# Two stage borders of a four-layer graph kernel are overlapped: load with the first similarity, the mix's last step with the last similarity

## The reference, cut to what matters

```python
# layers 0 and 3: xn is x transposed to (512, 64, 128)
x_norm = xn / jnp.maximum(jnp.linalg.norm(xn, axis=-1, keepdims=True), 1e-12)
mean_sim = jnp.einsum('nbl,mbl->nm', x_norm, x_norm) / B      # 512 x 512, summed over 64 batches
_, idx = jax.lax.top_k(mean_sim, k + 1)                       # k = 153 neighbours of each row are kept
A = jnp.where(mask, mean_sim, 0); An = dinv[:, None] * A * dinv[None, :]
out = jnp.einsum('sd,sbl->dbl', An, jnp.einsum('nbl,lo->nbo', xn, weight)) + bias
...
# layer 1: tokens are mixed by adj * adj; layer 2, for each batch of 128 tokens:
A_l = relu(zn @ zn.T) * not_eye;  A_g = exp(-d2 / (2 sigma^2)) * not_eye     # both times adj, rows normed
out = (w_l * K_l + (1 - w_l) * K_g) @ v @ W_O.T
```

## Time and profile before

| what | us |
|---|---|
| device time, median of 3 runs (1420.53 to 1422.23) | 1421.34 |
| the profiled execution, device time | 1420.99 |
| its span on the core | 1419.3 |
| busy PE, of the span | 1313.2 |
| busy DVE | 1081.6 |
| busy ACT | 818.8 |
| busy POOL | 566.3 |

### The profile page before, as it was taken

How to read it: one execution, slowest core, us unless ns; L and a number is a source line. 1 busy time by engine, 2 the same in 40 slices (tenths; PEclk the granted TensorE clock), 3 DMA queues, 4 the chain that set the end, 5 groups by cost and what they waited for, 6 DMA issues and landing times. The chain is left out here.

```text
span 1419.3 us, 29584 instructions
## 1 busy us (share of the span) xinstructions
PE 1313.2 (93%) x8776; PEld 726.5 (51%) x8806; DVE 1081.6 (76%) x2169; ACT 818.8 (58%) x1366; POOL 566.3 (40%) x866
## 2 busy tenths in 40 slices
PE   6689988999999889999999999999947997999997
PEld 2156555555555345555555555555514567455553
DVE  0498777888888847888888888888788988356664
ACT  5634345787777633555555555555445446477776
POOL 2100114787787711222222222222222001688887
PEclk9999987999999889999999999999988998999999
DMA  8756200000000022112211111222205440122222
GB/s 325 266 189 210 89 0 1 1 0 0 0 0 0 12 49 38 38 38 38 38 37 37 37 37 37 43 39 39 36 13 177 161 136 1 45 90 81 81 81 97
DMA packets 122971, 93.62 MB, mean 66 GB/s; under 512 B 87712, under 2 KB 87840, under 8 KB 122912
## 3 DMA queue, kind: packets, MB, share of 16 engines
q1 hardware_dynamic: 122720, 92.81, 22.7%
q0 software_dynamic: 192, 0.08, 0.0%
HBM read 54.86 MB, written 17.04 MB: 51 GB/s over the span
## 5 line engine op out<-in xcount | busy, mean ns | idle before, releaser
L546 PE MATMUL pair<-unit_lo,unit_hi 128*128 128x512 f16 x512 | 178.8, 386 | 29.5 <-ACT unit_hi L617 24.7
L2030 POOL TENSOR_TENSOR sq_lo<-sq,sq_hi 128x512 f16<-128x512 f32 x60 | 69.6, 1160 | 139.2 <-ACT sq_hi L1803 139.2
L550 PE MATMUL diag<-unit_hi 128*128 128x128 f16 x512 | 113.4, 221 | 0.0
L548 PE MATMUL pair<-unit_hi 128*128 128x384 f16 (+2 forms) x384 | 106.4, 277 | 0.0
L1150 PE MATMUL po<-an_h,xwh 128*128 128x512 f16 x256 | 98.0, 383 | 0.0
L1151 PE MATMUL po<-an_l,xwh 128*128 128x512 f16 x256 | 97.9, 382 | 0.0
L1152 PE MATMUL po<-an_h,xwl 128*128 128x512 f16 x256 | 97.8, 382 | 0.0
L1785 PE MATMUL work<-m_h,xT 128*128 128x512 f16 x256 | 97.0, 379 | 0.0
L1786 PE MATMUL work<-m_l,xT 128*128 128x512 f16 x256 | 97.0, 379 | 0.0
L1787 PE MATMUL work<-m_h,xT 128*128 128x512 f16 x256 | 97.0, 379 | 0.0
L1089 POOL TENSOR_TENSOR x_all<-x_all,t 128x512 f32 (+1 forms) x64 | 81.2, 1269 | 16.8 <-ACT t L983 12.1
(11 more groups left out here) (438 smaller groups left out, 4237.7 us busy)
## 6 DMA issues: line engine op xcount, KB each, us to landing
x_all<-in_x_dram SPq DMA_DIRECT2D x16, 1024.0 KB, 14.5
tl<-rn_rows SPq DMA_DIRECT2D x64, 256.0 KB, 3.7
sim<-rn_rows SPq DMA_DIRECT2D x64, 256.0 KB, 3.7
out_dram<-x_all SPq DMA_DIRECT2D x64, 256.0 KB, 2.0
weights_a<-in_L_gnn_W_lang_dram SPq DMA_DIRECT2D x1, 1024.0 KB, 11.4
weights_b<-in_L_gnn_W_grav_dram SPq DMA_DIRECT2D x1, 1024.0 KB, 8.3
weights_a<-in_L_gnn_W_O_dram SPq DMA_DIRECT2D x1, 1024.0 KB, 10.6
an_h<-in_L_gnn_W_V_dram SPq DMA_DIRECT2D x1, 512.0 KB, 5.6
```

What stands on the lines that cost most here:

```text
L546: nc.tensor.matmul(pair[i][:], stat, lo[:, r, :], start=first, stop=False, skip_group_check=True)
L548: nc.tensor.matmul(pair[i][:, (i + 1) * P:], stat, hi[:, r, (i + 1) * P:], start=False, stop=final, skip_group_check=True)
L550: last = nc.tensor.matmul(diag[:, i * P:(i + 1) * P], stat, stat, start=(first and i == 0), stop=final, skip_group_check=True)
```

## The change

- **Load and the first similarity are one block** (`load_and_compare`), with no meeting between them. Of each of the parts 6 to 15, POOL squares one batch of four (as a product of x with itself). The root of the early scales is taken one part earlier. The rows of scales, wo, wv and wg are loaded in another order.
- **In both similarities (class `Similarity`) half of the lo parts, the odd batches of a round, go from DVE to POOL** (`lo_on_pool`).
- **The greatest sum (`greatest`) is found by POOL after its last lo part**; before it stood ahead of the middle of the similarity.
- **Step 16 of the mix becomes `closing`**: the 64 grams of layer 3 with the rest of the mix between them. The first four units and hi parts stand inside step 15, and so do the early scales (LATE = 3: groups 13 to 15 are late). The norm statistics of group 14 move from step 15 into closing, and its norm and squares stand behind the grams' rounds 4 and 5; group 15's outputs are PE's work ahead of round 5, its statistics stand around round 6, its norm and squares around round 7. Late scales are stored by SP instead of POOL.
- Buffers and banks are shared accordingly. The meeting with `release_semaphores` that stood between load and similarity and the one between mix and similarity go; one stands between layer 3's similarity and its neighbours, where before there was only the end of a block.

In the diff the last piece is DVE's order in the new step 16; where a line repeats what the list says it is left out.

```diff
-LATE = 2
+LATE = 3
...
+    def units(self, dve, base, start=False):
+        for r in range(self.R):
+            self.take_unit(dve, base, r, start)
+        for r in range(0, self.R, 2 if self.shared else 1):
+            self.lo_on_vector(dve, base, r, start)
...
+    def lo_on_pool(self, pool, base, start=False):
+        for r in range(1, self.R, 2):
...
+    def greatest(self, pool):
+        pool.wait_ge(self.late.top, 1)
+        pool.partition_all_reduce(self.k.s(NSQ_MAX), self.k.s(NSQ_MAX), P, RMAX).then_inc(self.gmax_all, 1)
...
+                early.store(sp)
+                early.all_stored(sp)
+                for base in range(0, B // 2, R):
+                    sim.load(sp, base)
...
+                def closing():
+                    ks = Kernels(NG - 1)
+                    for r in range(0, R, 2):
+                        sim.lo_on_vector(dve, 0, r, True)
+                    ks.add_turned()
+                    sim.units(dve, R)
+                    ks.mask_gravity()
+                    ks.sums()
+                    sim.units(dve, 2 * R)
+                    ks.factors()
+                    ks.mix()
+                    sim.units(dve, 3 * R)
+                    kernels_lo(NG - 1)
+                    moments(NG - 2, range(0, 2))
+                    sim.units(dve, 4 * R)
+                    moments(NG - 2, range(2, G))
+                    sim.units(dve, 5 * R)
+                    add_outputs(NG - 1, (pgg, pbc, pgg, pbc), range(G))
+                    dve.wait_ge(o_u, NG * G)
+                    last.moments(dve, range(0, 2))
+                    sim.units(dve, 6 * R)
+                    last.moments(dve, range(2, G))
+                    sim.units(dve, 7 * R)
...
+                    sim.units(dve, 9 * R)
+                    dve.wait_ge(last.sums, 1)
+                    sim.late.clamp(dve)
+                    sim.units(dve, 10 * R)
+                    sim.late.invert(dve)
+                    sim.units(dve, 11 * R)
+                    sim.late.refine(dve)
```

More of the change, by code:

```diff
@@ L467, in _ @@
                         mix.lang.sum_squares(pe)
+                pe.wait_ge(mix.lang.tmp_r, C)
+                pe.wait_ge(mix.lang.q_in, 1)
+                for r in range(R):
+                    sim.gram(pe, 0, r, r == 0, False)
+                with strided(pe, R, B - R, R) as base:
+                    sim.grams(pe, base)
+                sim.grams(pe, B - R, True)
             @block.vector
@@ L1615, in scratch_tiles, with kernel_mix @@
     return h[:, 0:N], h[:, N:2 * N], l[:, 0:N]
-def select_neighbours(k, rows_bank, scale, layer, mix, ops, ahead=None, last=None):
-    with ExitStack() as banks:
-        pair, diag = similarity(k, banks, rows_bank, scale, layer, mix, ops, ahead, last)
-        neighbours(k, pair, diag, rows_bank, ops, mix, ahead)
-def kernel_mix(k, w, rows_bank, head):
+def kernel_mix(k, w, rows_bank, head, work, pgl, pgg, ahead):
     nc, X, idle = k.nc, k.X, k.idle["dve"]
@@ new lines, in kernels_hi, with hi, closing @@
+                def kernels_hi(g):
+                    act.wait_ge(k_r, g + 1)
+                    nc.scalar.activation(k_hi, gs[:], ACT.Copy, scale=S_K).then_inc(kt_h, 1)
+                def hi(q):
+                    for r in range(R):
+                        sim.take_hi(act, q * R, r, q == 0)
+                def closing():
+                    exponential(NG - 1)
+                    hi(1)
+                    hi(2)
+                    kernels_hi(NG - 1)
+                    hi(3)
+                    hi(4)
+                    normalise(NG - 2)
+                    square(NG - 2, 0)
+                    hi(5)
+                    for j in range(1, G):
+                        square(NG - 2, j)
+                    hi(6)
+                    last.normalise(act)
+                    act.wait_ge(v_d, NG * G)
+                    act.wait_ge(o_d, NG * G)
+                    last.squares(act, range(0, 2))
+                    hi(7)
+                    last.squares(act, range(2, G))
+                    hi(8)
+                    hi(9)
+                    sim.late.take_root(act)
+                    for q in range(10, B // R):
+                        hi(q)
+                    sim.root_of_greatest(act)
@@ L1813, in step @@
                 def step(s):
+                    if closes(s):
+                        return closing()
                     if s.live(2):
[L1815 to L1820 removed]
+                        normalise(s.at(2))
@@ L1970, in step @@
                             lo(tg_lo[:, e, :], work[e][:], tg_hi[:, e, :], S_EVAC, tg_h, s.at(0) * C + e + 1, tg_l)
+                    if before_close(s, 1):
+                        early.invert(dve)
+                        add_outputs(s.at(1), work, range(0, 1))
+                        early.refine(dve)
                     if later(s):
```

686 lines of the change are left out of this document (393 added, 293 removed).

## The result

The changed kernel takes 1428.36 us (median of 5, 1427.63 to 1430.42), the kernel before 1421.22 us (median of 5, 1420.27 to 1422.23): a ratio of 1.0055, 95% interval 1.0044 to 1.0067. It is slower by 7 us, over the 2.8 us that can be told. Two executions that stand far above the others of their kernel, one of e9 at 2789.38 us and one of the kernel before at 1461.84 us, are left out of medians and ratios. The profiled execution has a span of 1425.9 us against 1419.3, so 6.6 us are to be found in the traces. I had forecast +1.6.

What follows compares the result with a forecast made beforehand. PE was taken to set the pace inside a similarity and stand still at the borders, with DVE almost full. Layer 0 at -4.8 us and layer 3 at +6.4 us summed to +1.6 us, 1423 us, range 1408 to 1435.

Steps and rivals of the forecast that it cites:

- T: In layer 3's closing, the end of group 14's statistics on DVE, put 33 us after 1041, at 1074.
- DVE idle for hi of rounds 5, 6, 7: In closing, DVE waits for hi parts behind ACT's norms and squares: 5.4, 2 and 7 us.
- contention in closing: In layer 3, 41 two-input POOL passes slow DVE by 27 us, with bounds of 0 and 38 us.
- Layer 0, first gram: At the end of the load, earlier stores and row loads bring the first gram to 60.7, 9.0 us earlier.
- Layer 0, the stretch: Layer 0's grams take 90.3 us plus 2.5 of low clock and 2.5 of PE waiting, ending at 156.0.
- A in layer 3: Case A, the layout holds (0.42): layer 3's grams start early but DVE sets their end; layer 3 costs 6.4 us.
- The row loads: At the load's end, stores land with x near 54, so row loads start at 54 instead of 60.89.
- Cover gone: none: Before layer 0's first gram, no cover is lost, since ACT is free from 54.
- Ten leave ACT for POOL: In the load, ten squares move to POOL, 5.2 us, so ACT and PE end near 54 to 55.
- B: Rival, chance 0.24: in layer 3 DVE keeps up, contention costs 12 us instead of 27; 1408 us.
- D: Rival, chance 0.23: in layer 3 all 41 POOL passes meet DVE, contention 38 us; 1434 us.
- Rival C: Chance 0.11: at both similarities' ends POOL prepares its search while waiting, each end 5 us shorter; 1413 us.

Runs made afterwards that it cites:

- e9: e6 with layer 0's late scales two rounds later on DVE and ACT's root moved with them; 1404.40 us.
- e4: The changed kernel with all squares of the load on ACT, none on POOL; 1427.23 us.
- e6: e5 with all squares of the load on ACT as in e4; 1403.54 us.
- e3: The changed kernel with ACT's order in closing altered: hi parts of rounds 5 and 7 ahead of the norms, squares redistributed; 1416.95 us.
- e1: The changed kernel with POOL's search ahead of the last two rounds, whose lo parts DVE makes, in both similarities; 1419.12 us.
- e7: The kernel before with only load and layer 0's similarity joined as in the changed kernel, mix and layer 3 as before; 1421.64 us.
- e2: The changed kernel with all lo parts of both similarities on DVE and POOL's search directly behind its late work; 1414.80 us.
- e5: The changed kernel with the edits of e2 and e3 together; 1406.89 us.
- e8: The changed kernel with the edits of e1 and e3 together, POOL keeping its lo parts up to round 13; 1406.89 us.
- e10: e9 with layer 0's first round on DVE mixing units and lo parts instead of four units, then four lo parts; 1403.74 us.

## Why the prediction was right or wrong

| step | predicted | measured |
|---|---|---|
| ACT and PE done with the load | 54 to 55 | 57.7 and 60.3 |
| stores, row loads, first unit | 48, 54, 57.2 | 50.56, 55.82, 58.99 |
| first gram, layer 0 | 60.7 | 64.75 |
| low clock in the stretch | 2.5 | 94.57 - 90.3 = 4.3 (before: 93.65 - 90.3 = 3.4) |
| PE's waits in it | 2.5 | 99.43 - 94.57 = 4.9 (before: 97.76 - 93.65 = 4.1) |
| last gram to next stage | 5.2 | 4.4 |
| clock behind it | 1.8 | 0.5 to the thresholds (9.95 against 9.48), gone by the mix |
| **layer 0 together** | **-4.8** | **+0.7** |
| first gram, layer 3 (less 0.66) | 1043 | 1044.1 |
| T, statistics of group 14 (less 0.66) | 1074 | 1074.3 |
| DVE idle for hi of rounds 5, 6, 7 | 5.4, 2, 7 | 5.27, 0.85, 6.31 |
| wait for the late scales | 1.5 | none |
| contention in closing | 27 | 24.1 |
| grams end (less 0.66) | 1168 | 1168.3 |
| last gram to next stage | 7.9 | 6.1 |
| clock behind it | 0.5 | 1.0 to the thresholds; 1.5 with the rest of the run |
| **layer 3 together** | **+6.4** | **+5.9** |

**Where it was wrong.** The steps that failed are "Layer 0, first gram" and the 2.5 and 2.5 us of "Layer 0, the stretch". The first gram came 4.0 us late and the stretch was 4.1 us too long; the end was 0.8 us shorter than I had it, and the 1.8 us of clock behind it did not last. That makes 5.5 us, and it turned "within 0.2%" into slower; the range held the time, and the case that came is A in layer 3 without the gain in layer 0.

- *The row loads*, 1.8 of the 4.0 us. I let the stores land with x at 54. x was through by then (DMA share 0.04 from 54 to 56), but the row loads were issued at 55.82, and e4 shows that an earlier issue of the stores doesn't change that. Why the stores land some 2 us behind x is not shown.
- *"Cover gone: none"*, the other 2.2 us: from the first unit to the first gram I had 3.5 us and it took 5.8. The weight's lo parts, 4.83 us on POOL, were pushed behind the last square and onto the first units: 3.65 us instead of 2.01. In e6 they lie ahead of them, and the first gram is at 62.65.
- "Ten leave ACT for POOL, 5.2 us, so ACT and PE end near 54 to 55." I priced the squares by ACT's time and left out the ring. A square on POOL holds its place for 1.04 us and PE's sum of it, and the next one must wait for that; a part takes 2.29 us, with ACT alone 2.15 (e4). I had no row of such a square before, and gave it no bound from above, though a POOL pass of 1.16 us stands in the earlier trace rows. The first gram doesn't wait for these sums; they reached it only through the order on POOL.
- *The stretch.* Its 5.0 us were too few by my own rows. In before the stretch is 97.76 us against 90.3 of grams, 7.5 us over, 3.4 of them clock and 4.1 waits (2.38 and 1.27 us behind the same late reciprocal and refine). The changed kernel has 9.1. So 2.5 of the 4.1 us were in the earlier trace rows to be read, and only 1.7 came with the change. Behind the second wait the granted clock is 0.83 over 10 us. e9 suggests that the place of the late scales hardly matters.

**Where it was right.** In closing T and both long waits are within about a microsecond, and so is the grams' end, this last in part by luck. From 1041.66 (my 1041) to DVE's last lo part at 1163.45 I had DVE busy for 108 us and idle for 16; it was busy for 103.7 and idle for 18.1, and the last products took 5.5 us instead of 3. The largest uncertainty, the 27 us of contention, measured 24.1; B (12 us) and D (38 us) both fell. e3, which changes the order of ACT and of what hangs on it, takes both waits away. The search at the end is shown by e1; its preparation took 5.9 us, not 7.0, in both layers. The Trainium skill (GPSIMD Engine Reference, section 2.1, Instruction dispatch), whose 6 us for the first call of a freshly loaded kernel I had set beside my 7.5, was the nearer here, though e1 has 7.09 and the earlier trace rows 7.02 us at the same instruction. My row was read beside a working DVE, and the search was to run at the end of a stage, where DVE is at rest: the seven searches at such an end (changed kernel, e3, e4, e7) have 5.76 to 5.94 us, those beside a working DVE 5.89 to 8.79.

**Rival C** was partly true, and I dismissed it too roughly. In e2 POOL waits at the search itself, for DVE's clamp, which ends at 1122.42 + 0.69 = 1123.11, and the search starts at once:

```profile
1123.25 0.70 POOL L472 PARTITION_ALL_REDUCE scalars<-scalars  x1 [12.97 <-DVE scalars L201]
```

So the preparation can lie inside a wait, if it is the search that waits. (In e9 it lies in one in part: POOL is free at 1102.18, the value is there at 1108.13, the search begins at 1108.92.) In the changed kernel POOL waits for the lo part ahead of it, and then it can't.

**Contention.** 24.1 us over 41 passes is 0.59 us of DVE for each, near the 0.66 that I took (27 / 41) and well under the price of the earlier trace rows (3.84 / 4 is 0.96, not the 0.94 that I wrote). The difference to e2 gives the same: 18.5 us over 32 lo parts, 0.58 each. Where the passes lie back to back, at 1110.16, the full 0.96 is paid; the rest of the time many miss each other. The mean is about what a lo part costs DVE itself (0.6 us), which fits e5 and e8 being equal. By the Trainium skill (GPSIMD Engine Reference, section 8, Key points) the two engines contend for SBUF interfaces, and the trace agrees in this; that all 41 passes would be charged in full, 38 us, is not what it shows.

What stays open: why POOL's preparation is longer beside a working DVE, why the stores land 2 us behind x, and which of the small differences among e6, e9 and e10 are real. Of the 1.5 us behind layer 3 in the changed kernel 1.0 is the clock; the other 0.5 is no more than the rest of the run differs by between kernels (248.96 us in e7, 249.31 in before, 250.79 in e1). e6's closing, in which DVE is busy 101.7 of 112.8 us, was not shortened further.

## What to carry to other kernels

Work handed to an engine that shares SBUF with the first may be worth nothing: 0.6 us of lo part saved, 0.6 us lost to contention, and the helper then stood in the way of other work (the search, the weight's lo parts). When two pipelines are laid into one queue, look at what stands *behind* each wait; two hi rounds behind two norms cost 11 us, and an order that changes no work won it back. Price a moved operation inside the ring it runs in, not by what it takes off the first engine. When a stretch is priced, start from what it costs over its bound now: 7.5 us stood in the rows, and I wrote 5.0. And keep instructions that need a preparation away from the last step of a stage, or let them be the ones that wait.

The best kernel here is e6, at 1403.54 us (ratio 0.9877, 0.9861 to 0.9892), with e9 and e10 not told apart from it: the two merged borders do pay, 1.2%, once the search stands early, POOL makes no lo parts or squares and ACT makes its hi parts first.

## What the runs showed of the hardware that I had not expected

- POOL's `partition_all_reduce` took 0.38 to 0.90 us in the two similarities, with 5.76 to 8.79 us of its own ahead of it each time that it followed a two-input pass or a store: 5.76 to 5.94 at the end of a stage (seven searches), 5.89 to 8.79 beside a working DVE. Where POOL waited for its data for longer than that, it began 0.14 us after they were there (e2, layer 3).
- DVE passes with two SBUF inputs beside POOL's: four took 6.33 us (1.58 us each against 0.62 alone) while POOL made four passes back to back.
- Behind a stand of PE of 6.08 us at a stage's end the granted clock was 0.77 for the ten microseconds from 1176, and four transposes took 0.94 to 1.12 us instead of 0.60 to 0.66. Up to the thresholds this cost 1.0 us (9.82 against 8.81); with a stand of 1.71 us (e1) it cost nothing (8.81).
